# The 16-feature attentions in two rounded fp32 parts, two heads at rows 0 and 64 of a stack, on Trainium2

## What is computed

```
# block 0: causal self-attention, and attention to the context, in one softmax
k = concatenate([k_self, k_ctx]); v = concatenate([v_self, v_ctx])
scores = einsum('bthd,bshd->bhts', q, k) * scale
scores = where((j >= t) | (j <= i), scores, -inf)
attn_out = einsum('bhts,bshd->bthd', softmax(scores), v)
...
# last block: attention to the context alone, with a mask over its 77 tokens
scores = einsum('bqhd,bkhd->bhqk', q, k)
scores = where(mask == 0, -1e20, scores)
out = einsum('bhqk,bkhd->bqhd', softmax(scores / 16), v)
```

## Time and profile before

| | |
|---|---|
| timed runs | 1905.60, 1909.23, 1910.78 us; median 1909.23 |
| the profiled execution | 1908.68 us, span 1906.9 us |
| TensorE busy | 1454.4 us (76%) |
| VectorE, ScalarE, GpSimd busy | 1084.3, 721.6, 505.9 us |
| mean granted TensorE clock | 0.85 of full |
| `at0`, from its first matmul to its last | about 92 to 455 us of the span |
| `at3`, the same | about 1663 to 1755 us |

### The profile page before, as it was taken

The page is one execution under the profiler, slowest core; times in us unless marked ns, Lnnn a source line. Parts: engine busy times, 40 slices in busy tenths (PEclk is TensorE's granted clock), DMA queues, the critical chain, the costliest instruction groups (busy, mean ns, idle before and its releaser), DMA issues. The chain is left out here.

```text
span 1906.9 us, 23196 instructions
## 1 busy us (share of the span) xinstructions
PE 1454.4 (76%) x7699; PEld 839.3 (44%) x7699; DVE 1084.3 (57%) x2383; ACT 721.6 (38%) x1013; POOL 505.9 (27%) x256
## 2 busy tenths in 40 slices
PE   5779998995398565677898957688896577588497
PEld 3424443331397323443444344344342466345396
DVE  5577776764633236535556164455553877575744
ACT  5215554556543212331333433123333232344554
POOL 3000000000300100211866820056686644200301
PEclk8859999998599767785999978679998787799699
DMA  6942222200000722183213004903300000550000
GB/s 227 250 84 48 48 48 49 48 2 1 0 1 2 200 45 92 45 276 89 47 39 71 1 1 155 243 11 78 78 1 23 0 1 1 131 99 3 0 12 34
DMA packets 85613, 123.16 MB, mean 65 GB/s; under 512 B 18772, under 2 KB 59126, under 8 KB 83702
## 3 DMA queue, kind: packets, MB, share of 16 engines
q1 hardware_dynamic: 85494, 121.66, 25.5%
HBM read 78.56 MB, written 42.48 MB: 63 GB/s over the span
## 5 line engine op out<-in xcount | busy, mean ns | idle before, releaser
L1150 ACT ACTIVATE x_feat<-banks,key_bias 128x1024 f32<-128x1024 f32 x168 | 185.2, 1113 | 341.3 <-PE banks L1058 281.8
L984 POOL TENSOR_TENSOR x_feat<-x_feat 128x1024 f32<-128x1024 f32 x112 | 265.5, 2371 | 89.1 <-ACT x_feat L1150 83.8
L1019 PE MATMUL banks<-stacks 128*128 128x512 f32 (+4 forms) x640 | 253.3, 430 | 47.0 <-DMA stacks<-k_parts_r 18.1
L1073 PE MATMUL banks<-x_feat,v_group 128*64 128x512 f32 (+4 forms) x1344 | 249.5, 585 | 19.6 <-DVE o_feat L1263 12.6
L1150 ACT ACTIVATE x_feat<-banks 128x1024 f32<-128x1024 f32 (+3 forms) x224 | 180.3, 839 | 141.9 <-PE banks L1052 92.9
L1193 DVE TENSOR_REDUCE max_parts<-banks 128x1 f32<-128x512 f32 (+3 forms) x384 | 192.9, 552 | 24.2 <-PE banks L1023 12.7
L1019 PEld LDWEIGHTS banks<-stacks 96*128 96x128 bf16 (+1 forms) x640 | 92.4, 148 | 225.2 <-DVE max_parts L1193 87.4
L1049 PE MATMUL banks<-stacks 99*128 99x512 bf16 (+3 forms) x512 | 139.9, 347 | 14.4 <-ACT x_feat L1150 5.9
L1057 PE MATMUL banks<-stacks 128*128 128x512 f32 x272 | 123.6, 454 | 18.8 <-DMA stacks<-neg_max_parts_r 18.8
L448 PE MATMUL banks<-ident,y_tok 128*128 128x128 f32 x224 | 44.5, 366 | 117.8 <-ACT y_tok L427 116.9
L1187 DVE CUSTOM_DVE_ANT_0 scratch<-banks,mask_rows 128x512 f32<-128x512 f32 x128 | 88.4, 690 | 67.4 <-PE banks L1019 67.3
(11 more groups left out here) (210 smaller groups left out, 2512.4 us busy)
## 6 DMA issues: line engine op xcount, KB each, us to landing
stacks<-q_parts_r SPq DMA_DIRECT2D x36, 512.0 KB, 9.1
stacks<-k_parts_r SPq DMA_DIRECT2D x24, 512.0 KB, 11.0
q_parts_r<-y_tok SPq DMA_DIRECT2D x18, 512.0 KB, 3.6
v_group<-v SPq DMA_DIRECT2D x14, 512.0 KB, 14.9
q_parts<-y_tok SPq DMA_DIRECT2D x16, 384.0 KB, 5.9
stacks<-q_parts SPq DMA_DIRECT2D x16, 384.0 KB, 4.9
k_parts_r<-y_tok SPq DMA_DIRECT2D x12, 512.0 KB, 6.8
w_even<-in_w SPq DMA_DIRECT2D x4, 1024.0 KB, 6.5
```

Of the source, the lines that this page charges most:

```text
L984: e.tensor_tensor(total, total, p, ALU.add)
L1019: m = e.matmul(PS[:, bank, at:at + wide], q[0:rows, h, qt * P:(qt + 1) * P], keys[0:rows, h, k0:k0 + wide], start=True, stop=not diag, ski ...
L1073: m = e.matmul(PS[w * h:w * (h + 1), bank, t.q0:CH], V[:, h, :], PB[:, t.index % 2, h // 2, h % 2, 0:CH - t.q0], start=t.first, stop=t.las ...
L1150: e.activation(dst, PS[:, 2 * (st % 2):2 * (st % 2) + 2, 0:CH - t.q0], ACT.Exp, scale=A.scale, bias=bias).then_inc(s.p_ready, 1)
```

## The change

For both 16-feature attentions:

- q and k are stored in two fp32r parts instead of three bf16 parts. VectorE does one subtraction for each item instead of three steps. The parts of 128 features x 512 tokens are 512 KB instead of 384 KB.
- A stack holds three blocks of 16 rows for a head (high x high, low x high, high x low), 48 rows, and two more for the negated maximum. The heads of even number start at partition 0, those of odd number at partition 64.
- The products for the maximum alternate between the two heads of a pair, and so do the scores. In the built program their tile of the array is now 64 x 128, at row 0 or 64. The masks keep 128 x 128.
- The products are cut differently: of the short blocks, (0,0) and (4,1), and (1,0) and (5,1), which are of equal width, share a chunk and are reduced by one VectorE operation; (2,0) and (6,1) stand alone. For each head that makes 10 chunks instead of 9, and 10 reductions instead of 12. The context comes in chunks of 4 query tiles of one head instead of 5 or 6.
- `send_rows` issues 8 small DMAs for a group instead of 3; a group's loads are 20 instead of 11 in `at0`, 6 instead of 3 in `at3`.
- `split_max` has three VectorE operations instead of five.

```diff
-Q_RUNS = [(0, 3), (0, 2), (0, 1)]
-K_RUNS = [(0, 3), (1, 3), (2, 3)]
-K16 = 96
-M_ROWS = 3
+Q_RUNS = [0, 1, 0]
+K_RUNS = [0, 0, 1]
+K16 = 48
+M_ROWS = 2
...
-    Q3 = dram("q_parts", (B * 2, 3, 16, 8, T), BF16)
+    Q3 = dram("q_parts", (2, B * 2, 16, 8, T), F32)
...
-            if parts == 3:
-                p2, p3 = (part(parts, it, i, k) for k in (1, 2))
-                step(e.tensor_tensor(r, r, p1, ALU.subtract))
-                step(e.tensor_copy(p2, r))
-                e.tensor_tensor(p3, r, p2, ALU.subtract).then_inc(s.split, 1)
-            else:
-                e.tensor_tensor(part(parts, it, i, 1), r, p1.bitcast(F32), ALU.subtract).then_inc(s.split, 1)
+            e.tensor_tensor(part(A, it, i, 1), RBUF[:, i % 2, 0:it.n], part(A, it, i, 0).bitcast(F32), ALU.subtract)\
+                .then_inc(s.split, 1)
...
-            n, size = A.nh * TB, 5 if self_keys else 6
-            A.chunks += [("ctx", i, min(size, n - i), 0) for i in range(0, n, size)]
+            if dh == 16:
+                A.chunks += [("ctx", h * TB + t, 4, 0) for k in range(A.pairs) for t in (0, 4) for h in (2 * k, 2 * k + 1)]
...
-                products = [[(i, 0)] for i in range(3, TB)] + [[(7, 1)], [(0, 0), (2, 0)], [(4, 1), (6, 1)], [(1, 0), (5, 1)]]
-            A.chunks += [("self", h, p, 0) for h in range(A.nh) for p in products]
+                products = [[(i, 0)] for i in range(3, TB)] + [[(7, 1)], [(2, 0)], [(6, 1)], [(0, 0), (4, 1)], [(1, 0), (5, 1)]]
+            A.chunks += [("self", 2 * k + hh, p, 0) for k in range(A.pairs) for p in products for hh in range(2)] if dh == 16 else \
+                [("self", h, p, 0) for h in range(A.nh) for p in products]
...
+    def rows16(h, n):
+
+        return slice(64 * (h % 2), 64 * (h % 2) + n)
...
-                        m = e.matmul(PS[:, bank, at:at + wide], q[0:rows, h, qt * P:(qt + 1) * P],
-                                     keys[0:rows, h, k0:k0 + wide], start=True, stop=not diag, skip_group_check=True)
+                        m = e.matmul(PS[:, bank, at:at + wide], q[rows(h), at_q(h), qt * P:(qt + 1) * P],
+                                     keys[rows(h), at_q(h), k0:k0 + wide], start=True, stop=not diag, skip_group_check=True)
...
-                    rows = K16 + M_ROWS * (not A.window)
+                    rows = rows16(h, K16 + M_ROWS)
                     k0 = 0 if t.kind == "ctx" else P + t.j * P
-                    m = e.matmul(o, k[0:rows, head_of_k(A, r, h), k0:k0 + P], q[0:rows, h, qs], start=True, stop=not t.diag,
+                    m = e.matmul(o, k[rows, head_of_k(A, r, h), k0:k0 + P], q[rows, h // 2, qs], start=True, stop=not t.diag,
                                  skip_group_check=True)
...
-                at = 0
-                for qt, half in qt:
-                    wide = min(CH, (qt + 1) * P - half * CH)
-                    m = e.tensor_reduce(maxp[:, h, qt, half:half + 1], PS[:, bank, at:at + wide], AX.X, ALU.max)
-                    at += wide
-                m.then_inc(s.chunk_free, 1)
+                first, n = 3 * (h * TB + qt[0][0]) + qt[0][1], len(qt)
+                wide = min(CH, (qt[0][0] + 1) * P - qt[0][1] * CH)
+                e.tensor_reduce(MXP[:, first:first + 13 * (n - 1) + 1:13], PS[:, bank, 0:n * wide].rearrange("p (j w) -> p j w", j=n),
+                                AX.X, ALU.max).then_inc(s.chunk_free, 1)
```

More of the change, by code:

```diff
@@ L544, in project_scalar, with project_vector @@
                 e.wait_ge(s.stored[i % 4], 16 * (i // 4))
[L545 to L556, removed]
-        if parts == 3:
-            for v in VT[1:min(4, sum(len(x[1]) for x in sections))]:
+            e.activation(part(A, it, i, 0), PS[:, i % 4, 0:it.n], it.func, bias=it.bias).then_inc(s.first_part, 1)
+    def project_vector(e, s, sections, A, relu):
+        vw = 32 if A.dh == 16 else 64
+        hv = D // A.dh
+        if A.dh == 16:
+            for v in VT[0:min(4, sum(len(x[1]) for x in sections))]:
                 e.memset(v, 1.0)
-            step(e.memset(VT[0], 1.0))
+            e.drain()
         def value(v, i):
@@ L633, in project @@
     def project(stage):
-        return sems(stage, ProjectSems, 16)
+        return sems(stage, ProjectSems, 15)
     def q_items(b, w, off, dst, bias, func, diag=False):
@@ L726, in attention @@
         if ctx_keys and not window:
-            n, size = A.nh * TB, 5 if self_keys else 6
-            A.chunks += [("ctx", i, min(size, n - i), 0) for i in range(0, n, size)]
+            if dh == 16:
+                A.chunks += [("ctx", h * TB + t, 4, 0) for k in range(A.pairs) for t in (0, 4) for h in (2 * k, 2 * k + 1)]
+                if self_keys:
+                    A.chunks[-1:] = [("ctx", 3 * TB + t, 2, 0) for t in (4, 6)]
+            else:
+                A.chunks += [("ctx", i, min(6, A.nh * TB - i), 0) for i in range(0, A.nh * TB, 6)]
         if self_keys:
@@ L742, in attention @@
             A.loads = 4
-        A.first_loads = (4 if dh == 16 else 7) * (not self_keys)
+        A.first_loads = 7 * (not self_keys)
         A.constants_kept = constants_kept
@@ L1772, in _ @@
         nxt()
-        project_sync(e, p0, sections0, 3, False, at0)
+        project_sync(e, p0, sections0, False, at0)
         nxt()
@@ L1810, in _ @@
         nxt()
-        project_sync(e, p3, sections3, 3, False, at3)
+        project_sync(e, p3, sections3, False, at3)
         nxt()
@@ L1906, in _ @@
         nxt()
-        project_scalar(e, p0, sections0, 3)
+        project_scalar(e, p0, sections0, at0)
         nxt()
@@ L1935, in _ @@
         nxt()
-        project_scalar(e, p3, sections3, 3)
+        project_scalar(e, p3, sections3, at3)
         nxt()
@@ L1952, in _ @@
         nxt()
-        project_vector(e, p0, sections0, 3, False)
+        project_vector(e, p0, sections0, at0, False)
         nxt()
@@ L1980, in _ @@
         nxt()
-        project_vector(e, p3, sections3, 3, False)
+        project_vector(e, p3, sections3, at3, False)
         nxt()
```

144 lines of the change are left out of this document (68 added, 76 removed).

## The result

The changed kernel takes **2398.74 us** (median of 4 runs, 2397.41 to 2401.65) against 1907.41 us (4 runs of the kernel before beside it, 1905.14 to 1910.78): a ratio of 1.2584, 95% interval 1.2556 to 1.2612. The profiled execution spans 2395.9 us, 489.0 more than before, at a mean clock of 0.71 against 0.85.

A forecast was written before the change was run, and what follows sets the result against it. TensorE's time was taken to decide in `at0` and `at3`. First stretch +11, `at0` +93 and +150, `at3` +150, projections -7 gave +397 on 1908.7: 2305 us, 80% range 2110 to 2430.

The forecast's parts named there:

- `at3`: Last attention stage: taken at half clock throughout, 28 us a group, +19 each, +150 us for eight groups.
- The price of a switch: Masked products on TensorE: changing tile for a 128-row mask adds 0.29 us at full clock, 0.42 at half.
- Pairs side by side: Unmasked products and scores of two heads run at once: 20 pairs, -4 us an `at0` group at full clock.
- A group at 0.50: One `at0` group at half clock takes 102 us, +60: 41 us doubled to 82, plus 20 for emptying the array.
- The clock in `at0`: Mask switches leave the array empty, so 2.5 of eight groups' time runs at half clock: 2.5 x 60 = +150 us.
- the clock never rises: Rival: half clock throughout `at0` and `at3`, +634 us, 2543 us in all; chance 0.07.
- the first stretch: `at0` before its first maximum, half clock: masks +13.4, context +4.5, pairs -1.7, absorbed idle 4.8; +11 us.
- +93 and +150: `at0` terms: 5.5 groups at full clock, 16.9 us more each, and 2.5 at half clock, 60 more each.
- VectorE's work: In `at0`, fewer reductions and `split_max` steps save some 1.5 us a group; TensorE's wait for VectorE goes, -1.6.
- Row maxima: Small row DMAs and loads in `at0` have a group's time to land: nothing, at most +3 us on the first group.
- Projections: VectorE's three-step chain and stalled bf16 cast go, stores grow by a third: -5 us block 0, -2 the last.
- The rival on idle gaps: Only TensorE's idle gaps lower the clock and the change adds short ones: clock holds, +229, 2138 us; chance 0.19.

## Why the prediction was right, and where it was wrong

The side and the range held; the measured time lies 94 us above the forecast. That it is inside the range is in part luck. The groups of `at0` took 111 us more than they were charged, because the clock stayed low, and it is no more than that only because the prices for half clock were too high; `at3` took 27 us less than it was charged.

- **The price of a switch: right.** Full clock, 384 columns: 0.53 against 0.22 in one mode (from 223.85 to 224.07 in the rows below, of the kernel before with merged blocks), so +0.31; forecast +0.29. Half clock: 0.94 against 0.54, +0.40; forecast +0.42. With bf16 weights a masked product is 0.10 cheaper, against the 0.11 that the prediction took for the load in the open.

```profile
223.85 0.33 PE L1049 MATMUL banks<-stacks 99*128 99x384 bf16 x1
224.02 0.22 PE L1052 MATMUL banks<-causal_k_rows,ident_bf 128*128 128x128 bf16 x1
224.07 0.33 PE L1049 MATMUL banks<-stacks 99*128 99x384 bf16 x1
```

- **Pairs side by side: right**, 8.1 us a group at half clock.
- **A group at 0.50: 102 forecast, 90 measured.** The prediction's own terms add up to 105: 82 and 20, and the 3 us of waits that it took as fixed and then left out (measured 3.4, TensorE's idle time in seven groups, by seven). It also doubled the load in the open (0.11 to 0.22, where its rows at half clock gave 0.16), so that the group at 0.50 holds 0.48 us for a mask, not 0.42. With heads one after the other masks cost (97.7 - 70.4) / 64 = 0.43 us each, of which 0.11 are the mask's columns: 0.32. By this 64 masks were charged 10 us too much. The clock was 0.53 and not 0.50, which is some 5 us of a group at full clock, and those would have taken 10. Together that is the 15 us between 105 and 90, by estimate. Why a mask costs 0.32 on average and 0.40 in the rows above is open: part of the weight loads may have stood in the open already without a mask (argued, not tried).
- **The clock in `at0`: wrong, and the step that failed.** I took 2.5 of eight groups at half clock because I asked only what the switches do to it. For the switches alone that was near the truth: the forecast's mix of 2.5 groups of 102 us and 5.5 of 58.5 is a mean clock of 0.78, and the kernel before with its masks on 64-row tiles ran at 0.78 in its profiled run. I never asked what a product of 48 rows does to it. It does more: 0.96 to 0.53 with no mask in the kernel. The rows that I read for the clock all had products of 96 and 99 rows. So the rival that I gave 0.07, the clock never rises, is what happened but for some 5 us in a group, behind the unmasked tiles and V. Its price of 2543 was too high by 12.7 us in each of seven groups (60 against 331.1 / 7 = 47.3), by 27 in `at3`, and by 37 in the last group. That group prepares no maximum for a next one: all 256 masks behind products have run by 757.1 us, before the last maximum at 760.3. The prediction charged 32 of them in the first stretch and 32 in each of eight groups, 32 too many. In the sum +93 and +150, together +243, stand for what measured 331 + 23 = +354.
- **`at3`: right in kind**, 0.50 throughout; +122.6 against +150, 25.3 us a group against 28. It grows from 86.0 us to 208.6, 2.4 times (its last matmul before the change starts at 1748.8 us, not near 1755). That the rows alone bring its clock to 0.60 is seen above; the forecast put the 0.50 down to the switches.
- **The first stretch**: +13.5 against +11. The unmasked pairs gave nothing there. Nine products of 512 columns follow each other every 0.79 us, (7.09 - 0.79) / 8:

```profile
95.95 7.09 PE L1018 MATMUL banks<-stacks 48*128 48x512 f32 x9
```

  VectorE reduces two of them in 1.41 us and then waits 0.16 for the next:

```profile
97.64 1.41 DVE L1191 TENSOR_REDUCE max_parts<-banks 128x1 f32<-128x512 f32 x2 [0.16 <-PE banks L1018]
```

  There are two banks for blocks, and a bank's turn is 0.79 us of TensorE, then 0.69 of VectorE and some 0.10 of handing over, 1.58 in series: with two banks, one product every 0.79.
- **VectorE's work: wrong, and without effect.** It was to fall by some 1.5 us a group and rose by 1.4 (226.87 / 7 against 217.31 / 7). The merged reductions alone saved 0.5 at full clock, and the kernel before became slower by them, not 1.6 us a group faster.
- **Row maxima: wrong in reason.** I had them land within a group's time, at most +3 once. The first wait is +2.8 (8.0 us against 5.2). But the maximum stands three tiles ahead of the group's end, not a group, and TensorE waits in each:

```profile
PE banks L1048 <- DMA stacks<-neg_max_parts_r: 17.5, 7, 7.7
```

  17.5 us in seven waits (view of the waits, 133 to 760 us: sum, times, longest), of which the six later ones, 9.8 us, were unforeseen. SyncE takes 5.53 us for the eight small sends, where the kernel before took 1.88 for three; that these 3.65 us more make the wait longer was not tried alone.

```profile
134.36 5.53 SPq L919 DMA_DIRECT2D stacks<-neg_max_parts_r  x8
```

```profile
126.31 1.88 SPq L928 DMA_DIRECT2D stacks<-neg_max_parts  x3
```

- **Projections: right in size**, -4.8 and -1.9 against -5 and -2. VectorE's subtraction takes 0.69 us each time and no cast stalls behind GpSimd. In the last block TensorE gains more than that and waits for it again: its waits for VectorE's splitting (2.3 and 1.3 us) are gone, but between its last projection matmul and the first product it stands 18.7 us instead of 13.7. No run has the projections alone.
- **The rival on idle gaps**: by the Trainium skill ("TensorE: Matmul & The Clock Gate", HAM oscillation) it is gaps that bring the clock down. The traces don't agree for this case: with 48 rows and no masks TensorE is busy 10.00 of 10.00 us and the clock is 0.50. In five groups of `at3` in the changed kernel it is busy 126.40 of 126.40 us at 0.50 as well, but there the busy time also covers the emptying of the array at each switch.

Put together, a group of `at0` went from 42.3 to 89.6 us: 22.6 by the switches at the masks, the other 24.7 by the rest, of which the low clock is the main part. Without the low clock the change might have paid: with masks on 64-row tiles TensorE is busy 61.5 us a group at a clock of 0.55, which is 61.5 x 0.55 = 34 us of full clock, and VectorE and ScalarE have 31.6 and 22.7. That is an estimate; no run has those products at full clock. No version that I ran beats the kernel before with the right result.

## What to carry to other kernels

Splitting TensorE's rows between two small matmuls gave two for the time of one here only where nothing of another tile stood between them; one 128-row mask after each product cost 0.3 us at full clock and 0.4 at half. Before that, ask what the clock will do: this kernel ran near its full clock and lost almost half of it by products of fewer rows, and then the saved work was worth less than the clock. Read the granted clock of a stretch together with the rows its matmuls use, not only with TensorE's busy share.

## What was unexpected of the hardware

- In `at0` the granted clock falls with the rows that matmuls use, at the same columns and with TensorE busy: 0.96 at 96 and 99 rows (bf16, no masks), 0.71 at 64, 0.53 at 48, and 0.51 at 48 and 50 in fp32r.
- Switches of tile without products of few rows also lower it: from 0.97 to 0.78 in `at0` of the one profiled run, the longer of two.
- A switch leaves both weight loads in the open: at 0.50, 0.29 us for fp32r and 0.11 for bf16.
- Adding 32 full-height matmuls to a group made two of seven groups shorter (63.2 against 67.0 us), since the clock came up to 1.00 in them; on average groups became longer (80.4).
- A VectorE reduction over two blocks saves little: eight merged pairs, 0.5 us, and the kernel before became 0.6% slower with them.
